# A two-layer graph kernel: buffers, instruction orders and load order of its first stage changed

## The reference, cut to what matters

```python
def _gat(h, adj, W, a, out_features):              # B = 16 items, N = 512 nodes, D = 128
    Wh = jnp.matmul(h, W)
    Wh1 = jnp.matmul(Wh, a[:out_features]); Wh2 = jnp.matmul(Wh, a[out_features:])
    e = jax.nn.leaky_relu(Wh1 + jnp.swapaxes(Wh2, 1, 2), negative_slope=0.2)
    scores = jnp.where(adj > 0, e, NEG)
    return jnp.matmul(jax.nn.softmax(scores, axis=1), Wh)
# layer 0: two rounds, residual, norm, feed-forward of width 512, norm
h = _gat(x, adj, W1, a1, 128); h = _gat(h, adj, W2, a2, 128)
h = _layernorm(x + h, g_ln1, b_ln1)
x = _layernorm(h + relu(h @ w_ff1 + b_ff1) @ w_ff2 + b_ff2, g_ln2, b_ln2)
# layer 1: attention of 8 heads, value weights chosen by the relation adj == r (r < 4)
q, k = x @ Wq + bq, x @ Wk + bk
out = sum((softmax(q k^T / 4) * (adj == r)) @ (x @ Wv[r] + bv[r]) for r in range(4))
x = _ln(x + out @ Wo + bo); x = _ln(x + gelu(x @ W1 + b1) @ W2 + b2)
```

## Time and profile before

| | us |
|---|---|
| median of 3 runs | 1168.77 (1168.24 to 1168.93) |
| the profiled execution | 1167.32 |
| its span, first to last instruction | 1165.5 |
| first stage, to the start of the second | 404.8 |
| DVE busy, share of the span | 940.0, 81% |
| PE busy, share of the span | 1067.7, 92% |

### The profile page before, as it was taken

How to read it: one execution, slowest core, us unless ns; L and a number is a source line. 1 busy time by engine, 2 the same in 40 slices (tenths; PEclk the granted TensorE clock), 3 DMA queues, 4 the chain that set the end, 5 groups by cost and what they waited for, 6 DMA issues and landing times.

```text
span 1165.5 us, 21832 instructions
## 1 busy us (share of the span) xinstructions
PE 1067.7 (92%) x6087; PEld 513.7 (44%) x6087; DVE 940.0 (81%) x2342; ACT 734.0 (63%) x1339; POOL 602.8 (52%) x506
## 2 busy tenths in 40 slices
PE   4699999999998689999999999999999999999995
PEld 3566766766755223333333333333333333244442
DVE  2888888888897778888978888889788888748777
ACT  3477787787785455656665666566656665654442
POOL 3332322322302068788878887888788877700000
PEclk9799999999999889999999999999999999999998
DMA  4321131131105033314331433143314320000000
GB/s 150 128 101 63 54 108 54 54 108 54 54 24 150 3 114 105 94 45 119 102 88 45 117 104 91 40 117 104 92 40 117 104 78 2 1 10 28 36 36 36
DMA packets 49547, 86.55 MB, mean 74 GB/s; under 512 B 8919, under 2 KB 35927, under 8 KB 44378
## 3 DMA queue, kind: packets, MB, share of 16 engines
q1 hardware_dynamic: 46586, 85.59, 23.9%
q10 hardware_dynamic: 2912, 0.40, 0.2%
HBM read 52.12 MB, written 29.36 MB: 70 GB/s over the span
## 4 chain that ended last, share of the span: by engine, by line
PE 52%; DVE 5%; POOL 3%; issue 3%; ACT 2%; ACTq 0%; POOLq 0%; DVEq 0%
PE b_o_ps L1302 18%; PE b_peak L1260 9%; PE b_score L1275 7%; PE b_peak L1852 4%; PE b_score L1844 3%; POOL b_picked L1765 3%; PE b_misc L1323 2%; PE b_misc L1313 2%; DVE top L1577 1%; PE b_misc L1338 1%; PE b_peak L1844 1%; PE b_misc L1322 1%; PE b_misc L1333 1%; ACT b_o_t L1433 1%; PE b_score L1837 1%
## 5 line engine op out<-in xcount | busy, mean ns | idle before, releaser
L1577 DVE TENSOR_REDUCE top<-b_peak 128x1 f32<-128x512 f32 x488 | 320.2, 684 | 75.3 <-PE b_peak L1260 73.8
L1422 ACT ACTIVATE b_prob<-b_score 128x1024 f32<-128x1024 f32 x256 | 257.8, 1025 | 156.9 <-PE b_score L1275 111.5
L1765 POOL TENSOR_TENSOR b_picked<-b_prob,mask 128x512 f32<-128x512 f32 x192 | 233.9, 1238 | 61.7 <-ACT b_prob L1422 48.5
L1765 POOL TENSOR_TENSOR b_picked<-b_prob,b_mask 128x512 f32<-128x512 f32 x185 | 226.2, 1243 | 55.7 <-ACT b_prob L1422 45.3
L467 POOL TENSOR_SCALAR a_code<-a_adj_in 128x512 bf16<-128x512 int32 x64 | 72.2, 1129 | 95.1 <-DVE a_xw_n L896 66.1
L1062 POOL TENSOR_TENSOR a_hw_n<-a_hw,a_inv 128x512 f32<-128x512 f32 x16 | 23.3, 1456 | 175.8 <-DVE a_inv L889 168.7
L833 ACT ACTIVATE a_att<-a_att,a_least 128x512 f32<-128x512 f32 x128 | 91.8, 720 | 31.3 <-DVE a_least L862 31.3
L1260 PE MATMUL b_peak<-b_k_stack,b_q_stack 96*128 96x512 bf16 x256 | 98.4, 384 | 6.9 <-DVE top L1577 6.5
L1260 PE MATMUL b_peak<-shared 96*128 96x512 bf16 x232 | 90.3, 390 | 10.2 <-issue 6.2
L862 DVE CUSTOM_DVE_ANT_0 a_att<-a_att,a_no_edge 128x512 f32<-128x512 f32 x128 | 88.7, 710 | 2.7 <-issue 2.2
L583 PE MATMUL a_turn<-a_hw_n,a_att 128*128 128x128 f32 x512 | 62.4, 281 | 17.6 <-POOL a_hw_n L1062 17.6
(11 more groups left out here) (240 smaller groups left out, 2033.1 us busy)
## 6 DMA issues: line engine op xcount, KB each, us to landing
a_adj_in<-in_adj SPq DMA_DIRECT2D x16, 1024.0 KB, 5.3
scratch<-shared SPq DMA_DIRECT2D x32, 384.0 KB, 2.7
shared<-scratch SPq DMA_DIRECT2D x16, 768.0 KB, 6.5
scratch<-shared SPq DMA_DIRECT2D x32, 256.0 KB, 2.1
b_q_stack<-scratch SPq DMA_DIRECT2D x8, 768.0 KB, 5.5
b_k_stack<-scratch SPq DMA_DIRECT2D x8, 768.0 KB, 8.2
a_x_in<-in_x SPq DMA_DIRECT2D x16, 256.0 KB, 2.7
xs<-in_x SPq DMA_DIRECT2D x16, 256.0 KB, 5.4
```

Source lines behind the costliest of these rows:

```text
L1422: act.activation(prob[s % 2][:, 2 * u:2 * u + 2, :], score[u][:, :, :], ACT.Exp, scale=float(DH) ** -0.5).then_inc(sem("exp_ready"), 1)
L1577: dve.tensor_reduce(top[g][:, hh, c:c + 1], peak[hh % 2][:, :], AX.X, ALU.max, negate=True).then_inc(sem("peak_read"), 1)
L1765: pool.tensor_tensor(picked[(NR * s + rel) % 2][:, hh, :], prob[s % 2][:, hh, :], m, ALU.mult).then_inc(sem("picked_pool"), 1)
```

## The change

It does these things, all in the first stage.

- `no_edge` has two buffers, used in turn. `edges(t)` moves from the scores of round one of item t (a step later) to step t itself, behind `invert(0, t-1)`. The loop body now holds two steps (`par` says which buffer), over steps 4 to 13; steps 14 and 15 are written out.
- `scale_rows` on DVE goes. POOL does it as `scale_x`, one instruction over 520 elements, behind `scale_hw` and ahead of `encode`. `see` moves to the end of the step, `invert(1)` behind the second mask of round one's scores, `add_h` ahead of the third mask, `invert(0)` behind `norm_stats(1)`.
- On PE, `turn_x` stands behind `turn_codes`, the four `feed_up` come in a row, `x_weights` follows the feed-forward, `turn_y` stands ahead of `round_two`, and `spread_row(0, t)` at the end of the step, behind `round_one`. ACT's list follows: `lower(0)` one step later, the copy of x_t behind the exponentials of round two, `s1_own` ahead of the copy of xw.
- Many groups of waits are written in another order, so that another wait of the group comes last.
- Value weights and biases (two loads) are issued once the first adjacency has landed, and `vector_late` runs first on DVE. Ten of the other loads follow item 1, then item 2 is loaded, then the last twelve. All engines wait for the late loads ahead of step 3, not 2.

```diff
-        no_edge = sb("no_edge", [P, C, N], BF16)
+        no_edge = [sb(f"no_edge{k}", [P, C, N], BF16) for k in range(2)]
...
             load(0)
+            sp.wait_ge(adj_loaded, 16)
+            prep.sync_values(sp)
             load(1)
-            prep.sync(sp)
-            with sp.Fori(2, B) as t:
+            prep.sync(sp, slice(0, 10))
+            load(2)
+            prep.sync(sp, slice(10, None))
+            with sp.Fori(3, B) as t:
                 load(t)
...
@@ tensor
-                if begin:
-                    turn_x(t)
                 if second:
                     spread_row(1, t - 2)
                 if feed:
                     turn_h(t - 3)
                 if begin:
                     turn_codes(t)
+                    turn_x(t)
...
                 if first:
                     pe.wait_ge(xw_ready, t + 1)
                     round_one(t - 1)
                 if feed:
                     turn_n(t - 3)
+                if begin:
+                    spread_row(0, t)
...
@@ scalar, a step
-                if begin:
-                    act.wait_ge(x_turned, t + 1)
-                    act.wait_ge(xw_done, t)
-                    act.copy(x_t[:, :], turn[:, :]).then_inc(x_t_ready, 1)
                 if second:
                     lower(1, t - 2)
+                if first:
+                    lower(0, t - 1)
...
+                if begin:
+                    act.wait_ge(xw_done, t)
+                    act.wait_ge(x_turned, t + 1)
+                    act.copy(x_t[:, :], turn[:, :]).then_inc(x_t_ready, 1)
                 if first:
                     exps(0, t - 1, range(C))
...
@@ vector, the waits ahead of a first leak
-                    dve.wait_ge(row_ready[k], b + 1)
-                    dve.wait_ge(low_ready[k], b + 1)
                     if k == 0:
                         dve.wait_ge(hw_done, b)
                         dve.wait_ge(s2_ready, b + 1)
+                        dve.wait_ge(edge_ready, b + 1)
                     else:
                         dve.wait_ge(round2_done, b)
                     dve.wait_ge(exp_ready[k], C * b)
+                    dve.wait_ge(row_ready[k], b + 1)
+                    dve.wait_ge(low_ready[k], b + 1)
                     leak(k, b, 0, s2)
...
@@ gpsimd
+            def scale_x(b):
+                pool.wait_ge(hw_done, b)
+                pool.wait_ge(inv_ready[0], b + 1)
+                settle(pool, w)
+                pool.tensor_tensor(xw_n[:, :, :], xw[:, b, :, 0:D + 2], inv[0][:, :].unsqueeze(2).to_broadcast([P, C, D + 2]),
+                                   ALU.mult).then_inc(scaled[0], 1)
```

More of the change, by code:

```diff
@@ L595, in round_one, with step @@
                 mm.then_inc(hw_done, 1)
-            def step(t, begin, first, second, feed, more):
-                if begin:
-                    turn_x(t)
+            def step(t, par, begin, first, second, feed, more):
                 if second:
@@ L1067, in _ @@
                 scale_hw(B - 2 + b)
+                if b == 0:
+                    scale_x(B - 1)
                 for n in range(2):
```

182 lines of the change are left out of this document (86 added, 96 removed).

## The result

| | before | changed |
|---|---|---|
| median of 12 runs, us | 1169.36 (1165.66 to 1172.40) | 1163.07 (1160.85 to 1165.49) |
| ratio, 95% interval | | 0.9947 [0.9936, 0.9958] |
| profiled execution, us (span) | 1167.32 (1165.5) | 1164.62 (1162.8) |
| K(0), K(1), K(14) | 41.66, 62.68, 340.69 | 44.67, 66.27, 337.48 |
| a step between K(1) and K(14) | 21.38 | 20.86 |

K(n) is the first leak of round two of item n, as in the prediction. The changed kernel is 6.3 us faster by the runs (1169.36 - 1163.07). The two profiled executions differ by 2.7 only: that of before lies 2.0 under its median, that of the changed kernel 1.55 over it. A difference of totals is therefore read from the runs, and its parts from distances that repeat in a trace, such as the 13 steps.

The account below looks back on a forecast made before the run. The prediction took a loop through the engines, with none full, to bound each first-stage step; +2.2 (opening) - 5.6 (13 steps) - 1.3 (tail) = -4.7 gave a span of 1160.8, 1162.6 with 1.8 around it, and 1164.0 us as median, range 1156 to 1173.

Parts of the forecast that it names:

- the middle: The 13 steady steps of the first stage: period from 21.38 to 20.95 us, 5.6 us saved.
- the opening: Start of the first stage up to the second K: first K at 44.9, second at 64.9, 2.2 us late.
- the tail: End of the first stage: no mask to make between the two rounds' scores, 1.3 us saved.
- the sum: Opening, steady steps and tail together: +2.2 - 5.6 - 1.3 = -4.7 us, leading to a median of 1164.0 us.
- the chain: Steady loop through the engines: reciprocal at K+12.42, scaling until K+14.6, round one at K+14.75, next K at K+20.8.
- R: Start of round one on PE, counted from K: K+14.45 before, forecast K+14.75.
- the hold: Steady step: DVE's mask and POOL's scaling exclude each other, so the scaling ends at K+14.6 instead of K+13.9.
- The rival without a hold: Steady step: mask and scaling don't exclude each other; period 20.25, sum -13.8, total 1155.0 us; chance 0.15.
- What follows is shifted as a whole: After the first stage, which ends at 404.8 us and holds all edits: the rest only moves in time.
- two end terms: Start and end of the first stage: 2.2 us late at the start, 1.3 us saved at the end.

Follow-up runs that it names:

- the mask last: The changed kernel with the making of the next mask moved to the end of DVE's step, behind norm_finish and ahead of see: 1164.38 us, ratio 0.9958.
- the mask buffer alone: The kernel before with only two mask buffers, a two-step loop body and the next mask made at the end of DVE's step: 1157.35 us, ratio 0.9905.
- the scaling on DVE: The changed kernel with round one's rows scaled on DVE again, right behind the reciprocal, instead of on POOL: 1167.34 us, ratio 0.9991.
- the idle transposes: The changed kernel with twenty transposes of a constant added on PE ahead of round one of item 0: 1162.49 us, ratio 0.9954.

## Why the prediction was right

The forecast was 1164.0 with a range of 1156 to 1173; the median is 1163.07. The mechanism of the middle held. That the total came within 1 us is in part luck, as the opening, the tail and the sum below show.

- **The middle.** Forecast 13 x (21.38 - 20.95) = 5.6 saved; measured 13 steps in 271.2 instead of 278.0, 6.8 saved, 20.86 a step. Every term of the chain stood: the reciprocal at K+12.47 (forecast 12.42), the scaling held until K+14.74 (14.6), R at K+14.88 (14.75), DVE's list and the lowered row as good as together (0.2 apart in the forecast). The step that carried it was to expect the hold, taken from the earlier trace rows. The run with the mask last confirmed that it is there (1.87 to 1.06), and the run with the mask buffer alone that taking the mask off the way to the reciprocal is enough to shorten the step.
- **What the middle left open.** The rival without a hold fell because the hold is there. Its price, a step of 20.25, was never measured: each edit that freed the scaling put the mask's 1.14 us somewhere else on DVE's list. With the mask last, `norm_finish` did end 0.86 earlier along with R, as that rival assumed. What the forecast didn't see is that POOL's scaling wasn't needed at all: with the scaling left on DVE the mask buffer alone gave 20.68.
- **The opening.** Forecast +2.2, measured +3.6. K(0), 44.67 for 44.9, was right by luck: round one of item 0 started at 35.63 instead of 37.1 (the second adjacency was issued at 15.30, not 16.6, and the forecast's own terms add up to 36.8) and took 6.82 instead of 5.6. The next step, forecast 20.0, took 21.60: round two of item 0 ran mostly at half clock (granted from 48.7 to 58.9 us; 5.92 at 54.48, against 3.81). It had taken 5.28 before, at 51.32, within a step of 21.02. The forecast took the terms of a steady step there and priced half clock for round one alone.
- **The tail.** Forecast 1.3 saved, measured 0.4 lost. The term as such was there, but round two of item 14 took longer. PE in the changed kernel, and in the kernel before:

```profile
347.95 5.44 PE L595 MATMUL a_turn<-a_hw_n,a_att 128*128 128x128 f32 x32 [2.01 <-POOL a_hw_n L1058]
```

```profile
352.88 3.81 PE L583 MATMUL a_turn<-a_hw_n,a_att 128*128 128x128 f32 x32 [3.38 <-POOL a_hw_n L1062]
```

The granted clock of the changed kernel in that stretch:

```profile
346.00:354.00 8.00, 6.05 (x40) 6.08 (x41) 4.09 (x11) 4.07 (x10) 3.87 (x4) 0.79 0.10 33
```

The clock fell to its lower level from 349.0 to 352.5, and the product lost 1.6 us: the size of the gain. In the run with the mask last the same product took 3.81 (at 347.67, granted clock 1.00), and K(15) came 21.7 us behind K(14), where it was 23.4 both before and in the changed kernel. So the term was right, and the clock took it.
- **The sum.** Forecast -4.7 at the start of the second stage; measured -2.8 there (404.79 to 401.99), and -2.7 in the two profiled executions. The median moved by 5.7 against the 1168.77 of the prediction. Thus the forecast was near the median with a middle term 1.2 too small and two end terms 3.1 too good, and with the profiled executions on different sides of their medians. The parts that a trace shows add up to 2.7 of the 6.3 us by which the runs differ; the other 3.6 are the distance of the two traced executions from their medians, and no run explains them. "What follows is shifted as a whole" held for this pair (760.7 and 760.8) and not in general: with the scaling on DVE it took 3.2 us more, with the mask buffer alone 1.3.
- **What stays open** is the opening. Three kernels had K(1) 2.8 to 3.5 us earlier in their traces than what they were built on, and no gain in the ratio that could be told from none. Whether untraced executions open differently, or the gain is given back in the part that the clock governs, no run here settles.

## What to carry to other kernels

A wait of one engine is free room only if the work put there doesn't hold up another engine that is busy in that time. Here a 0.6 us instruction in a 0.81 us wait of VectorE, beside GpSimd's encoding, made the kernel 0.4% slower, and the same kind of move where GpSimd was idle was part of a gain of 0.5%. Before a step is shortened, look at what two engines are doing in the same microseconds, and keep the phase that is good.

When a change has many parts, time the one that removes work from the loop alone. Here that part was worth 0.95% by itself, and the whole change 0.53%.

## What the hardware showed that was not expected

- A series of short VectorE instructions lost more than a single long one: the four of `norm_finish`, 1.11 us in the kernel before, took 2.63 in the middle of the encoding, as POOL's instructions got in between; a single mask held by a scaling took 1.24 instead of 0.68.
- With 3.4 us of idle transposes on PE just ahead of it, the next product ran at the upper clock (3.82 instead of 6.82 us).
- The granted clock in the profile's rows isn't complete at the start of a trace. For 28 to 34 us it reads 0.50 in the changed kernel and 1.00 in the run with the idle transposes, though the same product (`x_weights`) took 2.13 us at 30.4 in both, and 1.06 in a steady step. Durations of instructions were trusted over it:

```profile
28.00:34.00 6.00, 2.96 (x12) 2.25 (x10) 0.71 (x2) 5.72 (x12) 0.36 (x1) 0.50 0.67 239
```

```profile
28.00:34.00 6.00, 4.41 (x20) 4.01 (x19) 0.72 (x2) 5.71 (x12) 0.37 (x1) 1.00 0.65 240
```

- The stretch at the lower clock behind the pause between the stages was 13.7, 17.1 and 20.5 us long in the traces of the mask last, the changed kernel and the scaling on DVE, and the second stage took 759.8, 760.8 and 764.0 us.
